# A lightning-attention layer with 64 routed experts on one core: order of the first row loads, queue of the result stores, spread of a head's loads

## The reference

```
qkv = silu(xn @ w_qkv.T)                      # 16 heads of 128
per head, over blocks of rows, slope s:
  o_intra = (q @ k.T * decay mask) @ v        # inside a block
  o_inter = (q * q_decay) @ state             # from the blocks before
  state   = block_decay * state + (k * k_decay).T @ v
out  = rmsnorm(o) * norm_w
attn = (sigmoid(xn @ w_gate.T) * out) @ w_out.T

logits = xn @ router_w;  top 4 of 64 experts by logits + router_bias
routed = sum over a row's 4 experts of weight * (silu(xn@wg[e]) * (xn@wu[e])) @ wd[e]
shared = sum over 2 shared experts of (silu(xn@swg) * (xn@swu)) @ swd
```

## Time and profile before

| | |
|---|---|
| median of 3 runs | 1761.14 us (1757.54 to 1761.16) |
| profiled execution | 1762.04 us |
| its span, first to last instruction | 1759.4 us |
| TensorE busy | 97% of the span, 11705 matmuls |
| TensorE weight load busy | 86% |
| VectorE busy | 74% |
| ScalarE busy | 41% |
| GpSimd busy | 35% |
| SP's queue | 237120 packets, 200.52 MB |
| chain that ended last | PE 84%, DVE 5%, DMA 4% |

### The profile page before, as it was taken

The page is one execution under the profiler, slowest core; times in us unless marked ns, Lnnn a source line. Parts: engine busy times, 40 slices in busy tenths (PEclk is TensorE's granted clock), DMA queues, the critical chain, the costliest instruction groups (busy, mean ns, idle before and its releaser), DMA issues.

```text
span 1759.4 us, 34485 instructions
## 1 busy us (share of the span) xinstructions
PE 1711.2 (97%) x11705; PEld 1515.1 (86%) x11705; DVE 1308.9 (74%) x2590; ACT 720.3 (41%) x1331; POOL 608.0 (35%) x826
## 2 busy tenths in 40 slices
PE   6999999999989999999999999999999999999997
PEld 5888899899978888888888888889999999999997
DVE  7888788888666676666766667667888888876666
ACT  4333443434334444444444444443434343434332
POOL 2333155555333334333333333423323333210011
PEclk9999999999999999999999999999999999999999
DMA  6666444344468888888788788854444444331234
GB/s 218 216 216 232 139 138 149 128 146 134 136 210 251 241 248 247 255 250 243 243 249 245 241 250 252 257 176 131 135 118 127 121 126 129 117 108 49 79 102 132
DMA packets 283501, 316.01 MB, mean 180 GB/s; under 512 B 37696, under 2 KB 233280, under 8 KB 283328
## 3 DMA queue, kind: packets, MB, share of 16 engines
q1 hardware_dynamic: 237120, 200.52, 37.2%
q0 software_dynamic: 33792, 88.13, 16.8%
q10 hardware_dynamic: 12416, 25.17, 3.8%
HBM read 169.21 MB, written 144.46 MB: 178 GB/s over the span
## 4 chain that ended last, share of the span: by engine, by line
PE 84%; DVE 5%; DMA 4%; issue 3%; POOL 1%; ACT 1%; SPq 1%; DVEq 0%; ACTq 0%; POOLq 0%
PE bank L1242 7%; PE bank L1284 7%; PE bank L1243 6%; PE bank L1267 6%; PE bank L1244 6%; PE bank L1224 6%; PE bank L1222 6%; PE bank L1223 6%; PE bank L1287 6%; PE bank L1275 5%; PE bank L1307 4%; DMA rows_turned<-xz 4%; PE bank L1298 3%; PE bank L1296 3%; PE bank L1297 3%; PE bank L1315 3%
## 5 line engine op out<-in xcount | busy, mean ns | idle before, releaser
L579 POOL DMA_DIRECT2D xsT<-rows_turned x384 | 210.8, 556 | 383.8 <-DMA rows_turned<-xz 374.0
L1242 PE MATMUL bank<-wh,xh 128*128 128x256 f32 x1024 | 293.8, 287 | 0.0
L1244 PE MATMUL bank<-wh,xl 128*128 128x256 f32 x1024 | 289.1, 282 | 0.0
L1243 PE MATMUL bank<-wl,xh 128*128 128x256 f32 x1024 | 288.9, 282 | 0.0
L677 ACT ACTIVATE kv<-bank 128x512 f32<-128x512 f32 x256 | 153.1, 598 | 224.6 <-PE bank L1244 224.6
L590 POOL DMA_INDIRECT yk<-slot_y,pos x128 | 131.7, 1029 | 262.1 <-DVE xr L996 171.4
L1030 DVE STREAM_TRANSPOSE kz<-kv 128x512 f32<-128x512 f32 x127 | 90.2, 710 | 166.5 <-issue 149.7
L1242 PEld LDWEIGHTS bank<-wh,xh 128*128 128x128 f32 x1024 | 193.4, 189 | 19.2 <-issue 15.9
L1222 PE MATMUL bank<-xh,wh 128*128 128x512 f32 x512 | 208.9, 408 | 0.0
L1284 PE MATMUL bank<-sm,kv 128*128 128x128 f32 x1024 | 198.6, 281 | 8.5 <-DVE sm L1010 8.4
L1046 DVE SCALAR_TENSOR_TENSOR og<-tg,bank 128x512 f32<-128x512 f32 x128 | 87.9, 687 | 155.2 <-ACT o L703 155.2
(11 more groups left out here) (165 smaller groups left out, 3693.4 us busy)
## 6 DMA issues: line engine op xcount, KB each, us to landing
keys_turned<-kz SPq DMA_DIRECT2D x127, 256.0 KB, 3.0
kT_by_group<-keys_turned SPq DMA_DIRECT2D x508, 64.0 KB
slot_x<-zeros ACTq DMA_DIRECT2D x8, 3072.0 KB, 9.9
we<-wexp_in SPq DMA_DIRECT2D x192, 128.0 KB, 2.9
xs<-slot_x SPq DMA_DIRECT2D x96, 256.0 KB, 4.2
rows_turned<-xz POOLq DMA_DIRECT2D x96, 256.0 KB, 4.1
xsT<-rows_turned POOLq DMA_DIRECT2D x384, 64.0 KB, 3.3
slot_y<-ys SPq DMA_DIRECT2D x96, 256.0 KB, 3.0
```

The lines of the kernel that those rows point to most:

```text
L579: pool.dma_start(xsT[q % 2][b * TB:(b + 1) * TB, :, :, :].rearrange("p a k j -> p a (k j)"), xz_back[q % 2, b]).then_inc(xsT_loaded[q % 2] ...
L1242: pe.matmul(dst, lh, rh, start=(k == 0), stop=False)
L1243: pe.matmul(dst, lh, rl, start=False, stop=False)
L1244: mm = pe.matmul(dst, ll, rh, start=False, stop=(k == KD - 1))
```

## The change

Three edits. The wait for the scatters and the row loads of pairs 0 and 1 leave `first_pairs` for a function of their own, which SP runs in step 26 ahead of `store_keys(26)`; the weights of pairs 0 and 1 stay where they were, behind `load_keys(26)`. The store of `ys`, with its wait, leaves `pair_done` on SP and becomes `store_result` on ScalarE: for pair q0 behind `silu_q`, for pair q0+1 behind `result(q0+1)`. And of the three transfers of a head's part 3, `norm_w` moves to part 1 and the decay table to part 2.

```diff
@@ load_head, on SP
+                if part == 1:
+                    sp.dma_start(raw[:, WC + D:WC + D + 1], norm_w[h]).then_inc(raw_loaded, 16)
                 if part == 2:
                     sp.dma_start(w[:, :, 3 * HD:4 * HD], wgate[h]).then_inc(raw_loaded, 16)
+                    sp.dma_start(raw[:, WC + D + 1:], tab_dram[h]).then_inc(raw_loaded, 16)
                 if part == 3:
                     sp.dma_start(raw[:, WC:WC + D], wout[h]).then_inc(raw_loaded, 16)
-                    sp.dma_start(raw[:, WC + D:WC + D + 1], norm_w[h]).then_inc(raw_loaded, 16)
-                    sp.dma_start(raw[:, WC + D + 1:], tab_dram[h]).then_inc(raw_loaded, 16)
@@ first_pairs and pair_done, on SP
                 for q in range(2):
                     load_experts(q)
+
+            def first_rows():
                 for r in range(CH):
                     sp.wait_ge(scattered[r], 16 * TOPK * NT // CH)
                 for q in range(2):
...
                 if q + 2 < NPAIR:
                     load_experts(q + 2)
-                sp.wait_ge(ys_ready, q + 1)
-                sp.dma_start(slot_y_pair[q], ys[q % 2][:]).then_inc(y_stored[q % 2], 16)
@@ SP's loop over the steps
+                if s == EXPERT0 - 2:
+                    first_rows()
                 if 1 <= s < NSTEP:
                     store_keys(s)
@@ ScalarE
+            def store_result(q):
+                act.wait_ge(ys_ready, q + 1)
+                act.dma_start(slot_y_pair[q], ys[q % 2][:]).then_inc(y_stored[q % 2], 16)
+
...
                 if experts:
+                    store_result(q0)
                     silu_pair(q0 + 1)
...
                 if experts:
                     result(q0 + 1)
+                    store_result(q0 + 1)
```

## The result

The changed kernel takes 1752.63 us (median of 5 runs, 1751.69 to 1758.65) against 1759.91 us before (5 runs); the ratio is 0.9971, with a 95% interval of 0.9959 to 0.9983. So it is faster, by 7.3 us by the medians and 5.1 by the ratio (its interval: 3.0 to 7.2), and not by the 12 forecast. The profiled execution took 1752.27 us with a span of 1750.5, 9.8 us less than the profiled one of before.

The account below looks back on a forecast made before the run. TensorE, busy 1711.2 of 1759.4 us, was taken as the bound, except SP's issue order at stalls. 1762.04 − 7.0 (step 27) − 6.6 (later stalls) + 0.6 (returning) = 1749.0 us; own range 1747 to 1751, 8-in-10 range 1746 to 1754.

Parts of the forecast that it names:

- the reading of step 27: Step 27: SP issues the first expert rows late, VectorE waits 7.37 us, TensorE stalls; loading rows earlier saves 7.0 us.
- My 0.2 us for `turn_rows(1)`: Cost of `turn_rows(1)` now standing ahead of an accumulator copy; bounds 0 and 0.7 us, 0.2 taken.
- Rival B: Step 27 stays long as another wait takes the place; 1752.5 us with half kept, 1756 with all; chance 0.07.
- bound of 48.2 us: Whole program: the change can be about no more than the 48.2 us in which TensorE does not multiply.
- The lock of the descriptor generator: ScalarE's second store could hold off SP's first expert load by up to 0.52 us, losing half SP's gain.
- rival C: ScalarE's second store, before the keys' silu, delays each step; slower from 2.1 us per store; chance 0.03.
- the stall of step 34: Step 34: SP issues expert loads late, TensorE idles 1.67 us; SP would come 2.4 us earlier.
- so the 6.0 us idle should go: Steps 28 to 74: TensorE's idle time vanishes with the restart behind it, 6.0 to 7.0 us, 6.6 taken.
- the 0.6 us set for what may come back: Expert steps: stalls left over because the store's traffic now goes ahead of the expert loads, 0.6 us over all.
- the term of SP's saving: Expert steps: SP loses two store issues a step, 0.586 us each by the median, 1.17 us or more.
- rival A: The store takes back what it gives at the gate and up matmul; about 3 us gained there, 1752; chance 0.18.
- the added loads: Head loads moved to parts 1 and 2 cost SP 0.5 us each there, less than the 1.17 given back.

Follow-up runs that it names:

- e14: Kernel before plus first rows ahead, expert numbers read before the wait, and result stores on ScalarE: 1750.81 us, ratio 0.9959.
- e1: The changed kernel with all three edits run again, no further edit: 1753.38 us, ratio 0.9962 to the kernel before.
- e9: Changed kernel, with SP reading both expert numbers of a pair before it waits for the down matmul: 1748.58 us, ratio 0.9937 to the kernel before.
- e8: Changed kernel, with ScalarE storing each result a second time into an unused tensor: 1774.05 us, ratio 1.0087 to the kernel before.
- e10: Changed kernel plus a second xz buffer, so VectorE does not wait for the previous pair's store: 1749.33 us, ratio 0.9939 to the kernel before.
- e5: Kernel before plus first rows ahead and head loads spread, result stores still on SP: 1751.21 us, ratio 0.9950.
- e4: Kernel before with only the spread: norm moved to part 1, decay table to part 2: 1759.10 us, ratio 0.9995.
- e7: Changed kernel, with ScalarE issuing the second pair's store only after the silu of the next step's values: 1749.35 us, ratio 0.9941 to the kernel before.
- e15: Kernel before plus first rows ahead and expert numbers before the wait, stores on SP behind the loads, second time: 1744.67 us, ratio 0.9930.
- e12: Kernel before plus first rows ahead, ScalarE stores with the second late, early expert numbers, two xz buffers: 1746.77 us, ratio 0.9925.
- e11: Kernel before plus first rows ahead and expert numbers before the wait, stores on SP, head loads as before: 1746.29 us, ratio 0.9923.

## Why the prediction was wrong

**Right:** the reading of step 27. Cause, place and price held in every kernel with the edit: 10.62 us against 17.80, no lower clock, the rows issued before 470.1, nothing late behind them. Forecast 7.0 us, measured 7.18. My 0.2 us for `turn_rows(1)` was not needed. Rival B is out. (The prediction's bound of 48.2 us for the whole change holds for idle time only: the slow tail, 1.6 of these 7.2 us, was busy time of TensorE.)

**Right:** ScalarE pays nothing for its issues (0.37 us each), which rules out rival C. The lock of the descriptor generator, of which the Trainium skill (Perfetto Trace Analysis, DMA Instruction — HWDGE) speaks, shows in no row: in e14 the issues of the 87 expert loads that overlap an issue of ScalarE's took 0.45 us by the median, the other 289 took 0.47.

**Right in its place:** the stall of step 34. SP came 2.11 us after `down` instead of 4.52, and steps 34, 42, 58, 66 and 74, which lost 3.8 us between them, lost 0.0 in the changed kernel.

**Wrong:** the step "so the 6.0 us idle should go", with the 0.6 us set for what may come back. The sum takes 6.6 − 0.6 = 6.0 us off the expert steps; they gave 1.65 us in the changed kernel's profile and nothing in e1's. The step took the seven stalls seen in one execution for all that there is to lose. Three things showed in the runs.

First, the term of SP's saving was too large. I reckoned 1.17 us a step; the loads of the second pair started 0.77 us earlier (2.25 to 1.48), because SP had not been late in all steps and cannot start before 0.74 us after `down`: until then it reads the expert number. That time, not in my sum, is what e9 took away.

Second, half of it came back, as in rival A, but not where A put it. The expert loads landed 0.4 us later after their issue, and the larger bill was the xz store, VectorE's wait on it (9.9 us in 13 waits against 5.9 in 9) and `sm` behind it. I had looked at TensorE's waits and gone back to SP from one of them. GpSimd's chain (store, landing, load) I named only in rival B, for step 27, although the full list of waits has it at the top (374.0 us in 96 waits). I also had VectorE's order wrong, with `sm` ahead of `turn_rows(q0+3)`; by that order a late xz store could hardly have held it up. e8, e10 and e14 show that this chain has next to no slack: with two buffers (e10) the `sm` waits are gone, and the expert steps take 679.82 us instead of e1's 684.25. GpSimd's busy share of 35% hides it, since the waiting for landings is not busy time.

Third, the spread did not remove a stall but moved it. I priced the added loads at 0.5 us a step, "less than the 1.17 that the stores gave back". Single issues of SP's are much longer than the rest (L415 in e5 above 1.31 us, L422 in step 50 1.54), and SP enters the next step late with two head loads in part 2 as it did with three in part 3 (e4, e5).

So of the three edits the first carries the gain, and the other two cost 3.4 us on top of it (1750.03 to 1753.38, same chip; 2.8 by the ratios). In the changed kernel itself the stores' share shows in the `sm` waits; the spread's is less clear there, since the steps with s mod 8 = 1 lost 0.9 us in its profile and 2.3 in e1's, against 0.1 before. Where the expert steps' stalls are gone altogether, with first rows and early numbers, the kernel takes 1744.67 to 1746.29 us, 3 to 4 us under my forecast. The forecast's idea of what there was to gain was about right, its means were not. Rival A, at 1752 with a chance of 0.18, was the outcome in its number, but in part by luck: the xz store, which carried most of the bill, is not in it.

Open: step 50 lost 0.7 to 4.0 us in all of the profiles of before, of the changed kernel and of e1 to e7, step 61 up to 1.5 in five of these nine, and neither in e15. In both the load of `wd` is issued slowly or lands late, and why just there no run tells.

## What to carry to other kernels

Before a transfer is moved to a second queue because its issuer is late, list what else is in flight at that time, and which of it has a waiting reader without slack: here a free engine, a free 0.37 us issue and the same bytes still cost 5 to 6 us where the store went out ahead of such transfers or among them (e14 against e15), and nothing that shows where the second one came later (e12 against e11, 0.5 us apart, with a second buffer besides). Look first for time in which the late issuer does something that it could do before its wait (here reading a register value), because that adds no traffic. And when loads are spread over steps, check the step after each new place, not only the one that was relieved.

## What the runs showed of the hardware

The granted clock stayed at 1.00 through step 27 when TensorE did not idle in it; before, after 5.54 us of idleness, it was 0.57 on average for 3.4 us, that is mostly at 1.2 GHz. This tail was a quarter of the 7.18 us.

A table read followed by address arithmetic costs SP 0.74 us before the first transfer of a pair and about as much before the second expert's; moved ahead of the wait, it took the four issues from 3.2 to 2.45 us.

With the DMA engines 0.80 to 0.82 busy, 256 KB more in each half step (e8; twice 0.26 MB on the 3.5 MB that a step of 14.2 us moves at 245 GB/s, so 15% more traffic and not the 7% of my expectation) cost 21 us against e1, and the same store issued by ScalarE, early, in place of SP, behind the loads, cost 6.1 us (e14 against e15; 5.1 by the ratios), at equal bytes. How much of this is the queue and how much the order no pair of runs separates. In e9 against e11, where the spread differs as well, the price was 2.3 us.
